# A two-block transformer on one core: experts fed with inputs scaled by the routing weight, and identity products on TensorE ahead of the second attention and in its first batch

## The reference, cut to what matters

```python
attn = softmax(where(mask, -inf, (Q @ K.T) * scale))     # 16 heads of 8 features
x = x + (attn @ V) @ Wo + bo
...
e = layernorm(x)                                          # no scale, no shift
logits = e @ Wg + bg
w, idx = top_k(softmax(logits), 2); comb = one_hot(idx) * (w / sum(w))
h = relu(e @ W1[k] + b1[k])                               # 256 hidden values
out = sum_k comb[k] * (h @ W2[k] + b2[k])
x = x + out
```

## Time and profile before

| | us |
|---|---|
| three timed runs | 239.51, 239.56, 242.68 (median 239.56) |
| the profiled execution | 237.72 |
| its span (first to last instruction) | 235.5 |

### The profile page before, as it was taken

The page is one execution under the profiler, slowest core; times in us unless marked ns, Lnnn a source line. Parts: engine busy times, 40 slices in busy tenths (PEclk is TensorE's granted clock), DMA queues, the critical chain, the costliest instruction groups (busy, mean ns, idle before and its releaser), DMA issues.

```text
span 235.5 us, 2445 instructions
## 1 busy us (share of the span) xinstructions
PE 170.0 (72%) x708; PEld 90.1 (38%) x708; DVE 162.8 (69%) x392; ACT 100.9 (43%) x183; POOL 88.7 (38%) x92
## 2 busy tenths in 40 slices
PE   0577740696737009478999899797898959999984
PEld 0333530342322007133323344334465736656652
DVE  5597999373377939744743622561699999999992
ACT  2138503333234000044525447545665664775751
POOL 3377024791079900000000000200397846966650
PEclk9999555599755555555755789979999997999999
...
DMA packets 6834, 7.23 MB, mean 31 GB/s; under 512 B 2318, under 2 KB 5798, under 8 KB 6822
## 3 DMA queue, kind: packets, MB, share of 16 engines
...
q10 hardware_dynamic: 564, 0.43, 0.6%
...
...
## 4 chain that ended last, share of the span: by engine, by line
PE 39%; DVE 36%; DMA 9%; ACT 7%; issue 7%; SPq 1%; POOL 0%; ACTq 0%; DVEq 0%
DVE prob L1364 6%; DVE nmax L1278 5%; PE bank L948 5%; DMA q_stack<-prob 4%; PE bank L951 4%; DVE stats L1105 3%; PE bank L845 3%; PE bank L882 3%; DMA wc_s<-in_w_ctx 3%; DVE a_n L1116 3%; PE bank L924 2%; DVE q_m L1180 2%; PE bank L1044 2%; DVE hid_l L1374 2%; PE bank L780 2%
## 5 line engine op out<-in xcount | busy, mean ns | idle before, releaser
L564 POOL TENSOR_TENSOR hid_l<-prob,hid_h 128x512 fp32r<-128x512 f32 x27 | 42.2, 1576 | 34.6 <-DVE hid_h L1367 31.1
L481 POOL TENSOR_TENSOR rstd<-vare,m_half 128x4 f32<-128x4 f32 x10 | 11.4, 1137 | 99.9 <-DVE vare L1110 96.5
L1278 DVE TENSOR_REDUCE nmax<-bank 128x3 f32<-128x462 f32 (+1 forms) x48 | 25.8, 581 | 20.2 <-PE bank L882 19.9
L693 ACT ACTIVATE prob<-bank 128x512 f32<-128x512 f32 x40 | 23.4, 597 | 28.0 <-PE bank L924 17.8
L882 PE MATMUL bank<-k_stack,q_stack 49*128 49x154 bf16 x128 | 21.0, 306 | 17.2 <-DMA q_stack<-prob 12.5
L1364 DVE TENSOR_TENSOR prob<-prob,w_s 128x512 f32<-128x512 f32 x32 | 29.8, 945 | 1.0 <-ACT prob L735 0.5
L882 PEld LDWEIGHTS bank<-k_stack,q_stack 49*128 49x128 bf16 x128 | 12.2, 121 | 36.2 <-DMA q_stack<-prob 14.1
L735 ACT ACTIVATE prob<-bank,col 128x512 f32<-128x512 f32 x32 | 21.5, 692 | 4.9 <-PE bank L1026 4.8
L780 PE MATMUL bank<-ident,a_n 128*128 128x128 f32 x40 | 8.2, 342 | 16.2 <-DVE a_n L1116 16.2
L924 PE MATMUL bank<-q_stack,k_stack 52*128 52x512 bf16 x32 | 15.3, 492 | 2.1 <-DMA q_stack<-nm_f 2.1
L1044 PE MATMUL bank<-hid_h,w_h 128*128 128x512 f32 x32 | 14.1, 440 | 1.5 <-DVE hid_l L1374 1.4
...
## 6 DMA issues: line engine op xcount, KB each, us to landing
...
w_s<-in_w SPq DMA_DIRECT2D x1, 1024.0 KB, 8.7
w_s<-in_w POOLq DMA_DIRECT2D x1, 1024.0 KB, 6.9
...
k_stack<-prob SPq DMA_DIRECT2D x12, 40.0 KB
...
```

What stands on the lines that cost most here:

```text
L564: pool.tensor_tensor(hid_l[:, g % NH], hid[:, g % NH], hid_h[:, g % NH].bitcast(F32), ALU.subtract).then_inc(hid_lo_pool, 1)
L693: nc.scalar.activation(prob[:, u % NPR], bank[RING[u % 4]][:], ACT.Exp).then_inc(prob_ready, 1)
L1278: dve.tensor_reduce(nmax[:, b, j, h0:h0 + nh], src.rearrange("p (h k) -> p h k", k=TK), AX.X, ALU.max, negate=True).then_inc(max_taken, 1)
```

## The change

**Experts.** The routing weight is applied to the input of an expert and not to its hidden values: VectorE multiplies the spread weights, read from PSUM, with e_f (`scaled`), ScalarE rounds the product (`scaled_hi`) and GpSimd subtracts (`scaled_lo`), once per step. This holds because the weights are not negative. b1 then must be scaled too. Since a layer-normed row sums to zero, feature 0 is minus the sum of the others: row 0 of each W1 is subtracted from all rows (four GpSimd instructions), row 0 becomes b1 by a DMA of 2048 single elements, and feature 0 of e_f is set to 1 by `one_row` once the gate has read it. The relu then reads PSUM and writes the rounded half at once (ScalarE), and VectorE makes the rest from PSUM and that half in one instruction (`hidden_lo`). The expert's input ring has NEC = 3 places. `up` is needed one step ahead of `down` and no longer two, and the tail pieces get new places, T_COMB of batch 0 in unit 37 and not 39. T_NEXT gives half of the second batch's last normalisation to ScalarE.

**TensorE.** `stream(n, b)` issues n products of the 128 x 128 identity with itself repeated to 512 columns (bf16). Nothing reads the results. 56 stand ahead of the wait for q_stack, one ahead of each of the first 12 groups of scores, 8 ahead of unit 0 and one in every even unit of the first batch.

```diff
 UNIT_PE = {1: (0, T_NORM0), 3: (0, T_NORM1), 4: (0, T_NORM2), 5: (0, T_NORM3), 7: (0, T_TURN), 9: (0, T_PROJ),
-           11: (1, T_NORM0), 13: (0, T_IN), 15: (0, T_GATE), 18: (1, T_NORM1), 19: (0, T_COMB), 21: (1, T_NORM2)}
-UNIT_ACT = {8: (0, T_PROJ), 13: (0, T_IN), 15: (0, T_GATE), 20: (0, T_COMB)}
+           11: (1, T_NORM0), 13: (0, T_IN), 15: (0, T_GATE), 17: (0, T_COMB), 18: (1, T_NORM1), 21: (1, T_NORM2)}
+UNIT_ACT = {8: (0, T_PROJ), 13: (0, T_IN), 15: (0, T_GATE), 18: (0, T_COMB)}
 UNIT_DVE = {1: (0, T_NORM0), 3: (0, T_NORM1), 4: (0, T_NORM2), 5: (0, T_NORM3), 9: (0, T_PROJ), 11: (1, T_NORM0),
             12: (0, T_IN), 15: (0, T_GATE), 16: (0, T_PICK), 18: (1, T_NORM1), 21: (1, T_NORM2)}
 
-TAIL_PE = {1: T_TURN, 2: T_PROJ, 4: T_IN, 5: T_GATE, 7: T_COMB}
-TAIL_ACT = {1: T_PROJ, 4: T_IN, 5: T_GATE, 7: T_COMB}
-TAIL_DVE = {1: T_PROJ, 2: T_IN, 4: T_GATE, 5: T_PICK}
-TAIL_LN = 2
+TAIL_PE = {(0, 1): T_TURN, (0, 3): T_PROJ, (3, 0): T_IN, (3, 2): T_GATE, (5, 2): T_COMB}
+TAIL_ACT = {(0, 1): T_PROJ, (2, 2): T_NEXT, (3, 0): T_IN, (4, 0): T_GATE, (5, 2): T_COMB}
+TAIL_DVE = {(0, 3): T_PROJ, (2, 2): T_IN, (3, 3): T_GATE, (4, 2): T_PICK}
...
             sp.dma_start(w1_s[:], w1.rearrange("e d h -> d e h")).then_inc(ld_w1, 16)
+            sp.dma_start(w1_first[:], w1[:, 0, :].partition_broadcast(P)).then_inc(ld_w1, 16)
...
                              mask_b[0:1, b:b + 1, :].broadcast_to([1, H, TKP])).then_inc(k_stacked[b], 16)
+            sp.wait_ge(w1_based, 4)
+            sp.dma_start(w1_s[0:1].rearrange("q e (c p) -> q (e c) p", c=HC),
+                         cols[:, C_B1:C_B1 + E * HC].rearrange("p (o v) -> o v p", o=1),
+                         allow_slow_non_contiguous=True).then_inc(ld_b1, 16)
...
                 add_rows(y_t, a_n, R_BO0, b, a_bo_ready)
+            pool.wait_ge(ld_w1, 32)
+            for k in range(4):
+                s = slice(2 * k, 2 * k + 2)
+                pool.tensor_tensor(w1_s[:, s], w1_s[:, s], w1_first[:, s], ALU.subtract).then_inc(w1_based, 1)
...
+            def scaled_lo(n):
+                pool.wait_ge(ec_hi, n + 1)
+                pool.tensor_tensor(ec_l[:, n % NEC], ec[:, n % NEC], ec_h[:, n % NEC].bitcast(F32),
+                                   ALU.subtract).then_inc(ec_lo, 1)
+
+            def one_row(b):
+
+                pool.wait_ge(logit_mm, b + 1)
+                pool.memset(e_f[0:1, b], 1.0).then_inc(e_one, 1)
...
-                act.wait_ge(ld_w1 if k < 4 else ld_w2, 16)
+                act.wait_ge(ld_b1 if k < 4 else ld_w2, 16)
...
+            def scaled_hi(n):
+                act.wait_ge(ec_ready, n + 1)
+                nc.scalar.activation(ec_h[:, n % NEC], ec[:, n % NEC], ACT.Copy).then_inc(ec_hi, 1)
+
+            def hidden(n, c):
+                g = n * HC + c
+                act.wait_ge(h1_mm, g + 1)
+                if g >= NH:
+                    act.wait_ge(y_mm, (g - NH) // HC + 1)
+                nc.scalar.activation(hid_h[:, g % NH], bank[RING[g % 4]][:], ACT.Relu).then_inc(hid_hi, 1)
...
+            def stream(n, b):
+
+                for _ in range(n):
+                    pe.matmul(bank[b][:].rearrange("p (r c) -> p r c", c=P), ident_b[:],
+                              ident_b[:].rearrange("p (o c) -> p o c", o=1).broadcast_to([P, NJ, P]),
+                              start=True, stop=True)
+
             def scores(n):
 
                 b, _, j, h0, nh = GROUPS[n]
+                if n < END[0][0]:
+                    stream(1, bank_of(n))
...
                 hq, i = UNITS[n]
+                if u == 0:
+                    pe.wait_ge(max_taken, END[0][0])
+                    stream(8, RING[0])
                 pe.wait_ge(nm_stacked[b][0], 16)
...
                     pe.wait_ge(prob_ready, u - 3)
+                if u < UPB and u % 2 == 0:
+                    stream(1, RING[u % 4])
...
-                pe.matmul(bank[XP[b][1]][:], pick_e[:, e], comb_f[:, b], start=True, stop=True)\
+                pe.matmul(bank[spread_bank(n)][:], pick_e[:, e], comb_f[:, b], start=True, stop=True)\
...
-            def down(n):
+            def up(n, c):
+                e, g = n % E, n * HC + c
+                if c == 0:
+                    pe.wait_ge(ec_lo, n + 1)
+                if g == 0:
...
+                g = n * HC + c
+                pe.wait_ge(hid_lo, g + 1)
...
 
+            stream(56, RING[0])
...
-            up(1)
+                if u in (UNITS_ALL, UNITS_ALL + 2):
+                    comb_spread((u - UNITS_ALL) // 2)
...
-                if n == E + 3:
+            comb_spread(2)
+            for n in range(NB * E):
+                for i in range(2 * HC):
+                    if (n, i) in TAIL_PE:
+                        tail(1, TAIL_PE[n, i])
+                    if i >= HC:
+                        down(n, i - HC)
+                    elif n + 1 < NB * E:
+                        up(n + 1, i)
+                    if i == (2 * HC - 1 if n + NEC == E else HC - 1) and n + NEC < NB * E:
+                        comb_spread(n + NEC)
...
                 elif piece == T_IN:
-                    ln_apply(LN_X3, b, x3, e_n).then_inc(e_ready, 1)
+                    ln_apply(LN_X3, b, x3, e_n, (NJ, NJ_DVE)[b]).then_inc(e_ready, 1)
...
-            def hidden(n):
-                for c in range(HC):
-                    g = n * HC + c
-                    h = hid[:, g % NH]
-                    dve.wait_ge(hid_full, g + 1)
-                    dve.wait_ge(comb_b_ready, n + 1)
-                    dve.tensor_tensor(h, h, comb_b[:, n % NCB], ALU.mult).then_inc(weighted, 1)
-                    if c == 0:
-                        dve.wait_ge(weighted, g + 1)
-                        dve.tensor_copy(hid_h[:, g % NH], h).then_inc(hid_hi[0], 1)
-
-            def hidden_lo(n):
-                for c in range(HC):
-                    if not lo_on_pool(n, c):
-                        g = n * HC + c
-                        dve.wait_ge(hid_hi[c], n + 1)
-                        dve.tensor_tensor(hid_l[:, g % NH], hid[:, g % NH], hid_h[:, g % NH].bitcast(F32),
-                                          ALU.subtract).then_inc(hid_lo_dve, 1)
+            def scaled(n):
+
+                b = n // E
+                dve.wait_ge(comb_b_mm, n + 1)
+                dve.wait_ge(e_one, b + 1)
+                if n >= NEC:
+                    dve.wait_ge(h1_mm, (n - NEC + 1) * HC)
+                dve.tensor_tensor(ec[:, n % NEC], bank[spread_bank(n)][:], e_f[:, b], ALU.mult).then_inc(ec_ready, 1)
+
+            def hidden_lo(g):
+                dve.wait_ge(hid_hi, g + 1)
+                dve.scalar_tensor_tensor(out=hid_l[:, g % NH], in0=bank[RING[g % 4]][:], scalar=0.0,
+                                         in1=hid_h[:, g % NH].bitcast(F32), op0=ALU.max, op1=ALU.subtract)\
+                   .then_inc(hid_lo, 1)
```

226 lines of the change are left out of this document (87 added, 139 removed).

## The result

The changed kernel took 247.24 us (median of four runs, 245.40 to 247.81) beside 239.53 us for the kernel before (median of four, 237.34 to 242.68). The ratio is 1.034, 95% interval 1.0243 to 1.0437. The forecast was 228.2 us and faster; the direction was wrong, and 247.24 lies outside the range of 221 to 236. The medians here are over all executions; as those of one kernel spread by 3% and more (237.3 to 245.3 us for the kernel before) while the clock rises and falls at other moments in each, every ratio and its interval compares only the faster timed executions of both kernels.

What follows compares the result with a forecast made beforehand. No engine was taken to bound the whole: VectorE bounds the experts, TensorE the first batch's units. 0.5 + 1.7 - 7.5 + 0 - 6.1 = -11.4 us gave 228.2 us, range 221 to 236 us.

Steps and rivals of the forecast that it cites:

- Term 1: W1 and b1 ahead of the first normalisations: b1 DMA lands at 34.2 us, just before ScalarE needs it; +0.5 us.
- the slower rival: Head: the b1 DMA runs on one engine, landing at 51.6 us; 244.4 us in all; chance 0.06.
- Term 2: The 56 identity products in the q_stack wait take 14.2 us over 12.5 us of cover: +1.7 us.
- Then twelve groups ... hide: Twelve score groups: each with its identity product takes TensorE 0.40 us at full clock, hidden under VectorE's maxima; no cost.
- Term 3: First batch's units of the second attention: full clock shortens them from 30.1 to 22.6 us, -7.5 us.
- The end "(15.9 + 2.1) x 2, about 36 us": First batch's units, slow end: clock at 0.50 throughout, about 36 us, +6 us.
- The first rival: First batch's units: clock rises in the wait, then falls; near 29 us, -1.5; 234.2 us in all; chance 0.17.
- The second batch and T_COMB: Second batch's units with the earlier routing-weight turn: TensorE's wait set against step 0's moved products; 0, ends -3.5 and +2.
- Term 4: Expert stage: VectorE loses SBUF work, TensorE becomes the bound, 56.7 us instead of 62.8; -6.1 us.
- the clock falls again: First batch's units: clock at 0.50 half of the time, -1.5 instead of -7.5 us; 234.2 us in all; chance 0.17.
- the late DMA: Head: b1's element-wise DMA lands past 34.9 us, each us later costing one; at 51.6 us, 244.4 us; chance 0.06.
- the T_COMB wait: Second batch's units: TensorE waits for VectorE's pick, 3.9 us with only about 2 us of unit work under it; taken as 0.

Runs made afterwards that it cites:

- identity alone: Kernel before plus only the identity products, in the changed kernel's places and numbers; experts, W1 and b1 as before: 252.83 us, ratio 1.051.
- contiguous row: Changed kernel with b1 in a DRAM array of its own, so the 8 KB go to partition 0 as one row: 242.80 us, ratio 1.017.
- half of b1: Changed kernel with the element-wise b1 DMA cut to four experts' 1024 elements, the other four left out: 243.48 us beside 243.06.
- ahead only: Changed kernel with late W1 roundings and, of the identity products, only the 56 before the q_stack wait: 235.87 us, ratio 0.979.
- The pair of runs on one chip: Changed kernel without identity products, W1 roundings late: T_COMB at 17/18 as changed, 231.36 us (0.966); put back to 19/20, 228.22 us (0.947).
- comb-back kernel: Changed kernel without identity products, W1 roundings late, T_COMB put back two units to 19/20: 231.45 us first, then 228.22 us, ratio 0.947.

## Why the prediction was wrong, step by step

**Term 1, the head: mis-sized, and it is the slower rival's place with another mechanism.** The step that failed is "2048 pieces over 16 engines take 2.6 us; on top comes the fixed part, at most the 2.84 us". The pieces took no more than was said; what comes on top of them is not fixed but grew with the elements, 9.0 us behind the engines' last work for 2048 of them and 4.2 for 1024. The order around it was right: ScalarE's roundings stand in front of the normalisation, and each us past 34.9 costs one. From a landing at about 39.5 that rule gives 4.6 us, and 6.4 us were measured against the execution's own head. The rival had a landing of 51.6 and a chance of 0.06. A DMA that no row shows, with 256 pieces to the KB where k_stack's has 3.2, deserved a wider upper end than 0.5 us, and moving four roundings would have covered it at any length.

**Term 2, the wait: right, in part by luck.** +1.7 us forecast, +1.7 measured; the 56 products took 14.2 us as worked out (ten at half the clock). But this held because the clock was at half when they began. In four of the seven profiles with the 56 (identity alone, contiguous row, half of b1, ahead only) it was full, they were through some 2.7 us before q_stack, and their cost stood in the groups instead. Wrong was "Then twelve groups ... hide": a group with its product took TensorE 0.62 us and not 0.40, so the maxima came 0.63 us apart (12 in 7.52 us) instead of 0.555; the nine products ahead of unit 0 took 4.02 us at half the clock over a cover of about 2 us, and ScalarE's copy waited for the second q_stack until 106.39, 1.2 us after the turn, which it also does in kernels without products. Together 3.5 us, where 0 stood.

**Term 3, the first batch's units: the sign was wrong.** The failed step is the choice of the full clock for all units. The text itself named the row that spoke against it (11.49 of 12.00 us busy at 0.50) and then trusted ten full-array products to change it. With ten the grant was 0.60 and the units 5.0 us longer. The end "(15.9 + 2.1) x 2, about 36 us" comes near the 35.13 measured, but by luck: it is for a grant of 0.50, and at the 0.60 measured the same sum gives 30 us, or 33 with the 2.7 of waiting. The 0.21 us for an identity product, from a row of products back to back, is too low among other work; with the clock at 1.00 and TensorE busy 28.92 of 29.22 us, 40 products and the 15.9 us of the rest make 0.33 us each (an estimate). The first rival's 29 us was too kind, as it let the clock be half for half the time. With the full clock really held, by 40 products, the formula gives 15.9 + 40 x 0.21 + 2.7 = 27.0 us, and 29.2 to 29.8 were measured.

**The second batch and T_COMB: 0 was wrong, +3.0 with the hand-over's +1.6 behind it.** The wait was computed (3.9 us over 2 us of other work, 1.98 measured) and then set against work that no longer stands in the units. The pair of runs on one chip prices the earlier turn at 3 to 4 us, since the clock falls behind the wait. How much of the +3.0 is the turn and how much the clock stays open: with late roundings and all identity products the same units took 27.03 us at a grant of 0.96, beside 29.67 at 0.79 here.

**Term 4, the experts: right in kind, too small.** VectorE's instructions on PSUM took 0.69 and 0.68 us (0.68 forecast), TensorE became the bound, steps are 3.30 us apart (213.07 to 216.37), 3.31 forecast:

```profile
L1360 DVE SCALAR_TENSOR_TENSOR hid_l<-bank,hid_h 128x512 fp32r<-128x512 f32 x32 | 21.6, 690 | 19.4 <-ACT hid_h L726 19.3
L1356 DVE TENSOR_TENSOR ec<-bank,q 128x512 f32<-128x512 f32 x15 | 10.3, 683 | 0.8 <-PE bank L1007 0.7
```

TensorE's idle time in the stage is 1.06 us of the 2.5 left for it. The other 2.5 of the 3.9 us lie, by subtraction, at its head, where the forecast took both kernels as equally far. VectorE is busy 37.66 us in it, less than the 45 forecast. The experts' new form, with T_COMB put back and the roundings late, is the 5% of the comb-back kernel; the change as a whole is this gain less what the rest cost.

**The chances.** 0.83 for faster rested on two terms, of which only the experts' had its durations in rows; the other hung on a clock of which the text itself said that no row shows it. The rival "the clock falls again", the late DMA and the T_COMB wait were each weighed alone; all three came, and none excludes another.
